# Cross-attention with both query tiles' scores in one stretch over four PSUM banks

## The reference, cut to what matters

```python
n = layernorm(x)                                   # 16 x 256 x 256
q = heads(n @ Wq); k = heads(ctx @ Wk); v = heads(ctx @ Wv)      # 8 heads of 64
attn = softmax(einsum('bhsd,bhld->bhsl', q, k) * 64 ** -0.5)     # 256 x 77 per head
x = x + einsum('bhsl,bhld->bhsd', attn, v) @ Wo + bo
x = x + ffn_ref(layernorm(x))   # 2 layers of local attention and a gated feed-forward
```

## Time and profile before

| | |
|---|---|
| median of three runs | 1418.66 us (1416.92 to 1420.14) |
| span of the profiled execution, first to last instruction | 1416.2 us |
| median less span (what lies around it) | 2.5 us |
| TensorE busy | 1385.3 us, 98% |
| VectorE, ScalarE, GpSimd busy | 77%, 66%, 54% |
| cross-attention, g=1 to g=15 | from 18.81 us to 231.03 us |
| g=16 and 17, mixed with the next stage | 231.03 us to 263.32 us |

### The profile page before, as it was taken

One profiled execution on the slowest core, in us unless ns is written; L12 is line 12 of the kernel. 1 busy time (PEld: TensorE's weight loads), 2 busy tenths in 40 slices (PEclk: granted clock), 3 DMA queues, 4 the chain that ended last, 5 costly groups with the idle time before them and its releaser, 6 DMA issues.

```text
span 1416.2 us, 32735 instructions
## 1 busy us (share of the span) xinstructions
PE 1385.3 (98%) x11563; PEld 1237.8 (87%) x11563; DVE 1090.6 (77%) x3067; ACT 935.8 (66%) x2662; POOL 761.9 (54%) x576
## 2 busy tenths in 40 slices
PE   8999999989999999999999999999999999999998
PEld 7999998778888888888888888888888888888887
DVE  5777776768788788888888878778778888888874
ACT  6877777456666666666666667666666666666662
POOL 1212222556566566666666667666656666666653
PEclk9999999999999999999999999999999999999999
DMA  5223122101100100010001211111111111111001
GB/s 190 90 92 110 48 67 90 47 20 29 30 30 30 30 29 28 28 28 28 28 29 29 71 29 37 33 35 37 37 37 37 36 36 36 36 36 37 29 30 31
DMA packets 50516, 63.41 MB, mean 45 GB/s; under 512 B 8402, under 2 KB 32104, under 8 KB 50408
## 3 DMA queue, kind: packets, MB, share of 16 engines
q1 hardware_dynamic: 50408, 61.99, 14.0%
HBM read 38.17 MB, written 16.78 MB: 39 GB/s over the span
## 4 chain that ended last, share of the span: by engine, by line
PE 65%; DVE 16%; ACT 9%; issue 5%; DMA 2%; POOL 1%; SPq 1%; DVEq 0%; ACTq 0%; POOLq 0%
PE pb L567 30%; PE pb L880 6%; PE pb L894 6%; PE pb L856 5%; PE pb L825 5%; PE pb L840 5%; ACT x_p L1079 4%; PE pb L920 4%; DVE p_t L1596 2%; DVE p_t L1610 2%; ACT x_pt L1085 2%; DVE r_sin L1583 2%; DVE n_sq L1562 2%; DMA x<-x 1%; DVE r_cos L1577 1%
## 5 line engine op out<-in xcount | busy, mean ns | idle before, releaser
L1823 POOL TENSOR_TENSOR n_inv<-n_cl,half_neg 128x16 f32<-128x16 f32 x64 | 211.2, 3299 | 178.2 <-DVE n_cl L1567 174.7
L1222 ACT ACTIVATE p_t<-p_t,s_nm 128x128 f32<-128x128 f32 (+1 forms) x512 | 227.0, 447 | 22.3 <-DVE s_nm L1596 20.9
L567 PE MATMUL pb<-h_hi,w_hi 128*128 128x256 f32 x704 | 207.5, 295 | 1.3 <-DVE h_lo L1558 1.2
L567 PE MATMUL pb<-h_hi,w_lo 128*128 128x256 f32 x704 | 198.7, 282 | 0.0
L567 PE MATMUL pb<-h_lo,w_hi 128*128 128x256 f32 x704 | 198.6, 282 | 0.0
L1828 POOL TENSOR_TENSOR r_cos<-r_cos,r_sin 128x1024 f32<-128x1024 f32 x64 | 154.6, 2415 | 53.8 <-DVE r_sin L1583 53.8
L1213 ACT ACTIVATE pt_t<-pb 128x512 f32<-128x512 f32 x192 | 114.3, 597 | 98.5 <-PE pb L840 97.8
L1178 ACT ACTIVATE qk_sq<-pb 128x512 f32<-128x512 f32 x128 | 72.5, 592 | 142.9 <-PE pb L567 141.5
L567 PE MATMUL pb<-wqkv_hi,xt_hi 128*128 128x512 f32 x384 | 163.9, 427 | 2.6 <-DVE r_sin L1583 2.3
L1859 POOL TENSOR_TENSOR hg_lo<-hg,hg_hi 128x256 fp32r<-128x256 f32 (+1 forms) x192 | 141.9, 760 | 44.5 <-DVE hg_hi L1627 44.5
L1596 DVE CUSTOM_DVE_ANT_0 p_t<-pb,mask_t 128x128 f32<-128x128 f32 (+1 forms) x512 | 151.9, 353 | 17.5 <-PE pb L825 17.3
(11 more groups left out here) (145 smaller groups left out, 3907.5 us busy)
## 6 DMA issues: line engine op xcount, KB each, us to landing
y_state<-x SPq DMA_DIRECT2D x32, 256.0 KB, 2.0
x_cur<-y_state SPq DMA_DIRECT2D x32, 256.0 KB, 2.6
x_res<-y_state SPq DMA_DIRECT2D x32, 256.0 KB, 2.8
x_in<-x SPq DMA_DIRECT2D x16, 256.0 KB, 2.9
x_state<-x SPq DMA_DIRECT2D x16, 256.0 KB, 2.0
x_orig<-x_state SPq DMA_DIRECT2D x16, 256.0 KB, 2.9
out<-x SPq DMA_DIRECT2D x16, 256.0 KB, 2.2
x<-x SPq DMA_DIRECT2D x32, 112.0 KB, 2.3
```

What stands on the lines that cost most here:

```text
L567: mm = pe.matmul(dst, s, m, start=(n == 0 and k == 0), stop=(n == len(pairs) - 1 and k == 2))
L1222: e = nc.scalar.activation(pu, pu, ACT.Exp, bias=s_nm[:, j, k:k + 1], scale=-1.0, accum_out=s_sum[:, j, k:k + 1])
L1823: nc.gpsimd.tensor_tensor(n_inv[:, t], n_cl[:, t], half_neg[:], ALU.pow).then_inc(pool_inv, 1)
```

## The change

The scores of both tiles are made in one call at the head of the iteration, tile 0 in banks 2 and 3, tile 1 in banks 0 and 1 (`XS_BANK`). The wait for the first exponentials is gone. Transposed probabilities go to banks 2 and 3, whose exponentials are done by then; for the last sequence (g=16) they go to banks 0 and 1, since `project` needs 2 and 3, and its units 0 and 1 then wait for the exponentials of units 2 and 3. The output product goes to bank 5, so the wait for the residual moves from unit 1's transposes to the second half of the queries, and g=16 has one before its first projection. On VectorE the maxima of unit 2 are taken right after the next input's statistics, those of unit 3 after the probabilities of unit 0, both ahead of the residual.

```diff
--- before.py
+++ after.py
@@ -358,6 +358,11 @@
         QT_BANK = [5, 4, 1, 2]
 
         FIRST_BANK = {(0, 0): 4, (0, 1): 5, (0, 2): 2, (1, 0): 2, (1, 1): 3, (1, 2): 4}
+
+        XS_BANK = [2, 3, 0, 1]
+
+        def xp_bank(b, u):
+            return u % 2 if b == SEQS - 1 else 2 + u % 2
 
         def is_first(n):
             return isinstance(n, int) and n == 0
@@ -594,29 +599,29 @@
                         mm = pe.transpose(pb[:, 4, c * T + t * P:c * T + t * P + P], xn[:, t, c * P:c * P + P], id_f)
                 mm.then_inc(x_tr, 1)
 
-            def x_scores(b, par, t):
-
-                if t == 0:
-                    pe.wait_ge(x_cq, at(b, 2, 2))
-                    pe.wait_ge(x_ck, IC * (b // GROUP + 1))
-                else:
-                    pe.wait_ge(x_exp, at(b, XUNITS, 2))
-                for k in range(4):
-                    for odd in range(2):
-                        r = odd * DH
-                        mm = pe.matmul(pb[:, 2 + odd, k * P:k * P + CTX], xq_t[r:r + DH, par, k, t * P:t * P + P],
-                                       xk_t[r:r + DH, b // GROUP % 2, k, b % GROUP * CTX:(b % GROUP + 1) * CTX],
-                                       start=True, stop=True)
-                        if k == 3:
-                            mm.then_inc(x_s, 1)
+            def x_scores(b, par):
+
+                pe.wait_ge(x_cq, at(b, 2, 2))
+                pe.wait_ge(x_ck, IC * (b // GROUP + 1))
+                for t in range(NT):
+                    for k in range(4):
+                        for odd in range(2):
+                            r = odd * DH
+                            mm = pe.matmul(pb[:, XS_BANK[2 * t + odd], k * P:k * P + CTX], xq_t[r:r + DH, par, k, t * P:t * P + P],
+                                           xk_t[r:r + DH, b // GROUP % 2, k, b % GROUP * CTX:(b % GROUP + 1) * CTX],
+                                           start=True, stop=True)
+                            if k == 3:
+                                mm.then_inc(x_s, 1)
 
             def x_probs(b, u):
 
                 pe.wait_ge(x_pn, at(b, XUNITS, u + 1))
                 if u >= 2:
                     pe.wait_ge(x_ptc, at(b, XUNITS, u - 1))
+                elif b == SEQS - 1:
+                    pe.wait_ge(x_exp, at(b, XUNITS, u + 3))
                 for k in range(4):
-                    mm = pe.transpose(pb[0:CTX, u % 2, k * P:k * P + P], x_p[:, u, k, :], id_f)
+                    mm = pe.transpose(pb[0:CTX, xp_bank(b, u), k * P:k * P + P], x_p[:, u, k, :], id_f)
                 mm.then_inc(x_ptr, 1)
 
             def x_values(b, par, t):
@@ -640,7 +645,7 @@
                 pe.wait_ge(x_olo, at(d, 2, 2))
                 for t in range(NT):
                     rows = slice(t * P, t * P + P)
-                    mm = split_product(pb[:, 1, t * D:t * D + D],
+                    mm = split_product(pb[:, 5, t * D:t * D + D],
                                        [(xo_hi_t[:, c, rows], xo_lo_t[:, c, rows], xo_hi[:, c], xo_lo[:, c])
                                         for c in range(IC)])
                 mm.then_inc(x_wo, 1)
@@ -650,6 +655,8 @@
                 if half == 0:
                     pe.wait_ge(x_thi, at(a, 1, 1))
                     pe.wait_ge(x_tlo, at(a, 1, 1))
+                elif a >= 2:
+                    pe.wait_ge(x_res1, at(a - 2, 1, 1))
                 for c in (2 * half, 2 * half + 1):
                     cols = slice(c * P, c * P + P)
                     mm = split_product(pb[:, 4 + half, (c % 2) * T:(c % 2) * T + T],
@@ -697,7 +704,7 @@
                     x_values_of(0)
                     return
                 if b is not None:
-                    x_scores(b, was, 0)
+                    x_scores(b, was)
                 if a is not None:
                     x_queries(a, 0)
                 if g == SEQS + 1:
@@ -710,18 +717,16 @@
                 if g == SEQS:
                     turn_x(0)
                 if b is not None:
-                    x_scores(b, was, 1)
                     x_probs(b, 0)
                 if g == SEQS:
                     pe.wait_ge(xt_zero, 1)
                     pe.wait_ge(w_lo, WEIGHT["w10c"])
+                    pe.wait_ge(x_res1, SEQS - 1)
                     project(0, None, 0, 1)
                 if a is not None:
                     x_values_of(a)
                     x_queries(a, 1)
                 if b is not None:
-                    if d is not None:
-                        pe.wait_ge(x_res1, at(d, 1, 1))
                     x_probs(b, 1)
                 if next_keys(a):
                     x_keys(*next_keys(a), 6)
@@ -1076,13 +1081,13 @@
                 if later(b):
                     act.wait_ge(x_ptr, at(plus(b, -1), XUNITS, u + 1))
                 for k in range(4):
-                    e = nc.scalar.activation(x_p[:, u, k, :], pb[:, 2 + u % 2, k * P:k * P + CTX], ACT.Exp,
+                    e = nc.scalar.activation(x_p[:, u, k, :], pb[:, XS_BANK[u], k * P:k * P + CTX], ACT.Exp,
                                              bias=x_nm[:, u, k:k + 1], scale=1.0, accum_out=x_sum[:, u, k:k + 1])
                 e.then_inc(x_exp, 1)
 
             def x_probs_copy(b, u):
                 act.wait_ge(x_ptr, at(b, XUNITS, u + 1))
-                nc.scalar.activation(x_pt[0:CTX, u].rearrange("p k n -> p (k n)"), pb[0:CTX, u % 2],
+                nc.scalar.activation(x_pt[0:CTX, u].rearrange("p k n -> p (k n)"), pb[0:CTX, xp_bank(b, u)],
                                      ACT.Copy).then_inc(x_ptc, 1)
 
             def x_queries_copy(a, par, half):
@@ -1371,7 +1376,7 @@
 
             def x_maxes(b, u):
                 dve.wait_ge(x_s, at(b, XUNITS, u + 1))
-                nc.vector.tensor_reduce(x_nm[:, u], pb[:, 2 + u % 2].rearrange("p (k n) -> p k n", k=4)[:, :, 0:CTX],
+                nc.vector.tensor_reduce(x_nm[:, u], pb[:, XS_BANK[u]].rearrange("p (k n) -> p k n", k=4)[:, :, 0:CTX],
                                         AX.X, ALU.max, negate=True).then_inc(x_max, 1)
 
             def x_inverse_sums(b, u):
@@ -1419,7 +1424,7 @@
                 dve.wait_ge(x_bias, at(d, 1, 1))
                 if later(d):
                     dve.wait_ge(x1_store, at(plus(d, -1), 16, 16))
-                nc.vector.tensor_tensor(x1_x.rearrange("p t d -> p (t d)"), pb[:, 1],
+                nc.vector.tensor_tensor(x1_x.rearrange("p t d -> p (t d)"), pb[:, 5],
                                         x_b[:, par].rearrange("p t d -> p (t d)"), ALU.add).then_inc(x_res1, 1)
 
             def y_stats(d):
@@ -1468,8 +1473,10 @@
                 if ahead:
                     x_stats(a + 1, 1 - par)
                 if b is not None:
+                    x_maxes(b, 2)
                     x_inverse_sums(b, 1)
                     x_norm_probs(b, 0)
+                    x_maxes(b, 3)
                 if g == SEQS + 1:
                     squares(0, 1)
                     clamp(0, 1)
@@ -1479,9 +1486,7 @@
                 if g == SEQS:
                     x_lo(0)
                 if b is not None:
-                    x_maxes(b, 2)
                     x_norm_probs(b, 1)
-                    x_maxes(b, 3)
                 if g == 1:
                     c_rests(1)
                 if ahead:
```

## The result

The change makes the kernel slower by a quarter of a percent: 1422.43 us median against 1418.66, ratio 1.0024 (95% interval 1.0017 to 1.0032). The prediction was 1415.0, in a range of 1412.5 to 1417.8. The profiled execution has a span of 1420.5 us, 4.3 more than before.

What follows compares the result with a forecast made beforehand. The prediction took TensorE as the bound, full in eight iterations, with gains only from stalls and shorter sequences: -2.2 - 0.8 - 0.4 - 0.7 + 0.4 = -3.7 us, so median 1415.0, range 1412.5 to 1417.8.

Steps and rivals of the forecast that it cites:

- Iterations without keys: g=13 to 15: the idle time before unit 3 is halved, 0.1 to 0.2 us gained in each, 0.4 in all.
- S+10.8: Iterations without keys: reckoned end of VectorE's last normalisation, in us after the scores' start S; used for the bound -0.3.
- The seams: TensorE, g=2 to 15: scores in one stretch save 0.16 us an iteration at the seams between products and transposes, 2.2 us.
- The stalls: g=3, 8 and 10: TensorE's stalls of 0.22, 0.74 and 0.18 us go, less a new 0.35 in g=8; 0.8 gained.
- The new stall for unit 0's probabilities in g=8: g=8: statistics start late at S+5.35, so TensorE waits for unit 0's probabilities; about 0.63 us, taken as 0.35.
- g=1: First iteration: waits for first exponentials and VectorE's last normalisation shrink; 0.7 us saved, bounds 0.2 and 0.9.
- g=16: Last sequence: first transposes wait for unit 2's exponentials, so projection and final output product come later; 0.4 us lost.
- Bank 5: Output product in bank 5: the residual's wait at its new place costs nothing, with 0.6 us of cover.
- The slower rival: Third maxima delay unit 0's probabilities, stalling TensorE 0.63 us in each of 14 iterations; 1423.8 us, chance 0.07.
- The seams give nothing: Rival: no gain at the seams, only 1.5 us remains, 1417.2 us; no measurable change, chance 0.37.

Runs made afterwards that it cites:

- e1: The changed kernel with VectorE's maxima of units 2 and 3 put back behind the residual; 1431.67 us, ratio 1.0094 to the kernel before.
- e9: The changed kernel with GpSimd adding the bias (x_b) to only 2 of each 256 columns from the third sequence on; 1416.54 us, ratio 0.9987 to before.
- e13: The changed kernel with VectorE's early aggregate (before the residual) and GpSimd's x_rs in front of x_b; 1413.18 us, ratio 0.9969 to before.
- e2: The changed kernel with VectorE taking unit 3's inverse sums and probabilities before normalising the next input; 1412.16 us, ratio 0.9954 to the kernel before.
- e10: The changed kernel with two extra unused statistics on VectorE in front of unit 3's inverse sums; 1439.30 us, ratio 1.0144 to the kernel before.
- e11: The same extra statistics as e10, added to e2's kernel behind the next input's normalisation; 1411.49 us, ratio 0.9966 to the kernel before.
- e3: The changed kernel with GpSimd computing the next input's deviation (x_rs) before x_b; 1428.76 us, ratio 1.0074 to the kernel before.
- e4: The kernel before, with only the output product moved to bank 5 and the residual's waits at their new places; 1416.95 us, ratio 0.9994 to before.
- e6: The kernel before, with VectorE taking unit 3's probabilities before the next input's normalisation; 1417.42 us, ratio 0.9989 to the kernel before.
- e12: The changed kernel with VectorE aggregating the next input's statistics right behind unit 3's maxima, before the residual; 1420.08 us, ratio 1.0021 to before.
- e5: The changed kernel's four banks, with tile 1's scores again behind the output product and VectorE's old order; 1419.88 us, ratio 1.0012 to before.
- e8: e2's kernel with ScalarE in g=16 taking unit 2's exponentials before rounding the next stage's input; 1411.12 us, ratio 0.9959 to the kernel before.

## Why the prediction was wrong

**The step that failed** is in "Iterations without keys": "VectorE's last normalisation, which I reckon ends at S+10.8" (unit 3's probabilities). It was used as a loose bound there and left out for the iterations with keys, where it decides. It ended at S+11.65 and TensorE wanted it at S+10.87; unit 3 was turned at S+11.70. That is 0.83 us of stall in each of g=2 to 12. In g=13 and 14, without keys, unit 3 was turned at S+11.7 too, against S+10.7 in g=15, which has no next input: 1.0 each. Together 11 us that the sum did not have. I had followed what moves on VectorE and ScalarE, and nothing on GpSimd.

The margin was small already. These are rows of g=12 in the kernel before:

```profile
183.37 0.23 DVE L1341 BATCH_NORM_AGGREGATE x_mv<-x_st 128x2 f32<-128x6 f32 x2
183.94 0.18 DVE L1379 RECIPROCAL x_inv<-x_sum 128x4 f32<-128x4 f32 x1 [0.33 <-ACT x_p L1079]
...
184.70 0.74 DVE L1362 TENSOR_SCALAR xn<-x_in,x_mv,x_rs 128x256 f32<-128x256 f32 x2
...
185.56 0.48 DVE L1383 TENSOR_TENSOR x_p<-x_p,x_inv 128x308 f32<-128x308 f32 x1
```
```profile
181.45 1.28 POOL L1788 TENSOR_TENSOR x_b<-x_in,bo_t 128x512 f32<-128x512 f32 x1 [9.95 <-DVE x L1422]
...
183.96 0.71 POOL L1784 TENSOR_TENSOR x_rs<-x_ve,half_neg 128x2 f32<-128x2 f32 x1
```
```profile
185.78 1.07 PE L619 MATMUL pb<-ones_at,x_p 128*77 128x128 f32 x8
```

Unit 3's probabilities were ready at 186.04, S+11.10, and TensorE began to turn them half-way through the eight, at about S+11.3. The change made TensorE want them 0.4 earlier, and they came 0.55 later. The 0.55 is made up of four differences between this iteration and g=12 of the changed kernel. The residual starts at S+6.54 and not at S+5.74: +0.80. The two maxima that stood behind it are gone: -0.76. Unit 1's probabilities hold VectorE 0.95 and not 0.54 us: +0.41. For x_b starts with the end of the residual; it lay beside statistics, a maximum and only the first 0.3 us of these probabilities, and now lies beside all of them. From the aggregate to the input's normalisation it takes 1.43 and not 1.33 us: +0.10.

The last of these hides a wait that I had put at nothing. GpSimd needs that 1.3 us for x_ve and x_rs in both kernels. Before, VectorE's own work and a wait of 0.33 for the exponentials of unit 2 covered it. The early third maxima end that wait, as forecast, but nothing is gained by it, for VectorE then waits 0.60 for x_rs; in e1, where the maxima are back, 0.32 for exponentials and none for x_rs. Against my S+10.8, two terms were thus missing: 0.55 for unit 1's probabilities beside x_b (e9) and 0.60 for x_rs (e13). The residual began 0.28 earlier than in my numbers (S+6.54, where an end at S+7.5 and 0.68 give S+6.82). The sum is S+11.67, against 11.65. How the 10.8 was made up is not in the prediction, so that this last sum comes out is no proof. That unit 3's probabilities set the iteration's end is shown by e2, e10 and e11.

The Trainium skill has the first term: "GPSIMD Engine Reference", Specifications, says that GpSimd shares its SBUF interfaces with VectorE and contends with instructions of VectorE that have two SBUF inputs or run in a 2-port perf mode. The trace agrees for the first kind: probabilities, with two SBUF inputs, go from 0.46 to 1.00 beside x_b, statistics beside it stay at 0.75. The input's normalisation, with one input tensor, also slowed in e3 (0.73 to 1.69); no run shows whether it is in such a mode.

**The seams** were there, but mis-sized: 0.33 us an iteration (14.16 to the 13.83 of e2, e11 and e13, where TensorE is full), where I took 0.16. The 0.16 at the output product's end is as read. The other 0.16 is in the stretch itself: 16 records take 1.05, 32 take 1.94, so starting a stretch costs 0.16, which I counted twice.
The Trainium skill's rule of drains at a change of tiling mode ("TensorEngine Tiling (Array Packing)", Tiling Modes), with the constant of a lone bf16 matmul in "TensorE: Matmul & The Clock Gate", Single matmul latency, gave an estimate of 0.33, nearer than my reading of the rows. The measured sum agrees; that a drain is what takes this time no run shows.

**The stalls** of g=3 and 8 did go as waits for copies and were replaced; that of g=10 went. The new stall for unit 0's probabilities in g=8, forecast as 0.35, came: g=8 is 0.35 longer than its neighbours (14.98 against 14.63), of which the trace shows 0.15 as idle time. It came in g=3 too, where none was forecast: 0.30, with the x rows 0.98 us late on VectorE. **g=1**: 0.7 forecast, 0.63. **g=15**, which has no next input, shows what was meant: 13.18 against 13.66, with 0.34 us of idling before unit 3 for the copy of unit 1. **g=16**: 0.4 forecast, 0.43, and 1.56 of clock on top in the profiled execution. **Bank 5**: free, as said (e4).

**The account** between the two profiles: g=2 to 14 +5.7, g=15 -0.5, g=1 -0.6, g=16 +2.0; the first scores start 0.9 earlier, ahead of anything changed, and what follows the final output product is 1.3 shorter, in unchanged code. Why these last two differ is not known; they show how far two profiles can be compared. Sum +4.3, the difference of the spans.

**The slower rival** had the right sign, and new waits of TensorE for x_p in many iterations came, which the prediction names as its mark. Its place was wrong: unit 0's probabilities are late in g=3 and 8 alone, and the maxima in front of them do more good than harm (e1). "The seams give nothing" is refuted by e2 against e6.

## What to carry over

When an instruction moves, follow what it releases on every engine, to the end of the iteration, and compare each arrival with the time at which the bound engine wants it; a chain beside a full engine may have only tenths of slack, as here 11 us came of it in 13 iterations. Order each queue by what the bound engine wants next: swapping two blocks of VectorE turned 0.24% slower into 0.46% faster. And when taking away one reason for a wait changes nothing, take away two before calling it innocent.

## What the runs showed of the hardware

One GpSimd instruction of 1.3 us (x_b, 128x512) slowed what lay beside it on VectorE by kind: probabilities (two SBUF inputs) 0.46 to 1.00, the input's normalisation 0.73 to 1.69 for its pair, statistics not at all (0.75). So x_b cost VectorE time while VectorE was not waiting for it, by what it lay beside.

The granted clock fell to its 1.2 GHz level behind 2.00 us of idling on TensorE in four profiles (the change, e2, e10, e11; about 3.5 us long) and did not behind the same 2.00 us in four others (e3, e9, e12, e13). It fell behind 2.70 us (e5) and 3.75 us (e1), and also behind 0.66 and 1.08 us close together (e8). In e10 it fell twice more, behind 1.93 us each time, and then stayed low for some 10 us with TensorE full. What makes the difference is open.
